# Graph network with slotted neighbours: 36 slots in five PSUM banks, norms computed on ScalarE

## What is computed

```python
def _genconv(h, edge_attr, src, dst, w1, b1, g1, bb1, w2, b2, t):
    msg = jax.nn.relu(h[src] + edge_attr) + EPS_MSG
    m = msg * t
    seg_max = jax.lax.stop_gradient(jax.ops.segment_max(m, dst, num_segments=N))
    ex = jnp.exp(m - seg_max[dst])
    denom = jax.ops.segment_sum(ex, dst, num_segments=N)
    alpha = ex / (denom[dst] + 1e-16)
    agg = jax.ops.segment_sum(msg * alpha, dst, num_segments=N)
    out = h + agg
    z = jax.nn.relu(_layernorm(out @ w1 + b1, g1, bb1))
    return z @ w2 + b2
...
for i in range(1, L):
    z = jax.nn.relu(_layernorm(h, ln_g[i], ln_b[i]))
    h = h + _genconv(z, e, src, dst, ...)
return jax.nn.relu(_layernorm(h, ln_g[0], ln_b[0]))
```

## Time and profile before

| | us |
|---|---|
| median of 3 runs | 6207.28 (6206.5 to 6214.1) |
| the profiled execution | 6218.0 |
| its span, first to last instruction | 6213.7 |
| VectorE busy | 4593.2 (74%) |
| TensorE busy | 4575.7 (74%) |
| GpSimd busy | 4185.6 (67%) |
| ScalarE busy | 2450.6 (39%) |
| mean granted TensorE clock | 0.827 |

### The profile page before, as it was taken

One profiled execution on the slowest core, in us unless ns is written; L12 is line 12 of the kernel. 1 busy time (PEld: TensorE's weight loads), 2 busy tenths in 40 slices (PEclk: granted clock), 3 DMA queues, 4 the chain that ended last, 5 costly groups with the idle time before them and its releaser, 6 DMA issues. The chain is left out here.

```text
span 6213.7 us, 106997 instructions
## 1 busy us (share of the span) xinstructions
PE 4575.7 (74%) x43556; PEld 3238.2 (52%) x43557; DVE 4593.2 (74%) x7210; ACT 2450.6 (39%) x3848; POOL 4185.6 (67%) x3850
## 2 busy tenths in 40 slices
PE   7715888999938777783777877468777756777786
PEld 6715777888825444452445544244544533454443
DVE  9431555444438999994899999489999957888887
ACT  2403566654513444441444443234434423333333
POOL 3054777766547777774777777377777747777775
PEclk8955888666669998896899889789988978898888
DMA  8971777665564555544455555445555534454552
GB/s 344 417 239 66 260 275 282 221 234 221 194 192 167 180 174 185 177 164 118 157 178 183 175 176 177 126 144 179 170 183 177 184 130 136 165 173 165 169 173 88
DMA packets 323285, 1168.13 MB, mean 188 GB/s; under 512 B 142130, under 2 KB 145380, under 8 KB 255444
## 3 DMA queue, kind: packets, MB, share of 16 engines
q1 hardware_dynamic: 172852, 890.91, 38.7%
q0 software_dynamic: 134800, 214.63, 13.7%
q10 hardware_dynamic: 15120, 55.50, 2.2%
HBM read 910.82 MB, written 249.92 MB: 187 GB/s over the span
## 5 line engine op out<-in xcount | busy, mean ns | idle before, releaser
L1258 POOL DMA_INDIRECT gb<-ztab,ovi x2704 | 2945.6, 1089 | 1025.3 <-issue 833.6
L1356 PE MATMUL bank<-ep_mid,keep 128*128 128x512 f32 (+3 forms) x3474 | 1568.1, 610 | 18.8 <-DVE ep_mid L1346 18.8
L1356 PEld LDWEIGHTS bank<-ep_mid,keep 128*128 128x128 f32 x3474 | 699.3, 203 | 853.1 <-issue 820.7
L1309 DVE TENSOR_REDUCE mx<-xb 128x64 f32<-128x2816 f32 (+17 forms) x196 | 1016.7, 5187 | 3.6
L1273 PE MATMUL bank<-zpw,oh_layers 128*128 128x64 bf16 x28812 | 879.7, 194 | 155.9 <-DMA zpw<-ztab 155.9
L1273 PEld LDWEIGHTS bank<-zpw,oh_layers 128*128 128x128 bf16 x28812 | 874.3, 98 | 211.1 <-DMA zpw<-ztab 156.9
L1096 POOL DMA_INDIRECT ecell<-zpw,ptg x588 | 646.8, 1100 | 228.1 <-issue 176.7
L1404 PE MATMUL bank<-keep,na 128*128 128x128 f32 x100 | 47.5, 475 | 952.8 <-DVE na L1401 952.8
L925 PE MATMUL bank<-byk,zpw 88*88 88x102 f32 (+13 forms) x4608 | 665.1, 332 | 53.0 <-DVE zpw L906 49.1
L925 PEld LDWEIGHTS bank<-byk,zpw 88*88 88x88 f32 (+13 forms) x4608 | 654.5, 234 | 62.8 <-DVE zpw L906 54.0
L1319 ACT ACTIVATE cm<-top_x,nt 128x64 f32<-128x64 f32 x196 | 68.2, 348 | 1501.4 <-DVE top_x L1313 1484.9
(11 more groups left out here) (222 smaller groups left out, 5784.6 us busy)
## 6 DMA issues: line engine op xcount, KB each, us to landing
oh_layers<-ohd SPq DMA_DIRECT2D x196, 1568.0 KB, 9.8
ea_in<-in_ea SPq DMA_DIRECT2D x101, 512.0 KB, 8.1
enc<-es_out ACTq DMA_DIRECT2D x101, 512.0 KB
cb<-rowc SPq DMA_DIRECT2D x49, 1024.0 KB
gb<-ztab,ovi POOLq DMA_INDIRECT x2704
...
```

The source lines that it names most:

```text
L1258: at["g"][d] = ga_l[d % 2](GP.indirect_dma_start(gb[d % 2][:, 64 * v:64 * v + 64], None, T["ztab"], bass.IndirectOffsetOnAxis(ap=ovi[:, i: ...
L1309: q = V(VE.tensor_reduce(mx[:, 0:64], x_of(d, 0, S.S[d]).rearrange("p (s f) -> p f s", f=64), AX.X, ALU.max))
L1356: q = PE.matmul(both[d % 2][:, 0:w], ident, rows[:, 128 * (c - a):128 * (c - a) + w], start=(c == 0), stop=(c + 4 >= S.S[d]), skip_group_c ...
```

## The change

Eight source blocks more get a slot of their own (23 singles and 13 pairs: 36 slots, in five groups of 8, 8, 8, 8 and 4) and the overflow shrinks: 628 overflow slots in all instead of 676, and 2392 slots instead of 2244 over the 49 tiles. All tiles have then 41 to 57 slots, tile 1 has 72. The groups use five PSUM banks; for the sums over the slots one bank is left, NA and NB share one, and the maximum `top_x` lies in the eighth. The encodings of the fourth group are added by an identity matmul of TensorE before the one-hot matmuls, and ScalarE copies the finished group into `xb`. The norm's arithmetic after the statistics is moved to ScalarE whole, with a table set that holds both Ln and Exp loaded at the start of a layer, and without gaps; the bias matmuls are issued after the waits for ScalarE. `pick` works in chunks of 6 slots. The diff, cut to its core:

```diff
@@ -50,12 +50,12 @@
 self.NN = 128 * self.ND
 assert self.ND == len(OVER) == len(EDGES) == 2 * self.pairs - 1

-self.singles = 15
+self.singles = 23
 self.groups = [(b, 1) for b in range(self.singles)]
 self.groups += [(b, 2) for b in range(self.singles, self.ND, 2)]
 self.G = len(self.groups)
 self.ones = [sum(n for _, n in self.groups[:s]) for s in range(self.G + 1)]
-assert self.ones[-1] == self.ND and self.G == 32
+assert self.ones[-1] == self.ND and self.G == 36

 self.sorted = [d // 2 if d % 2 else self.ND - 1 - d // 2 for d in range(self.ND)]
 self.place = [self.sorted.index(b) for b in range(self.ND)]
...
@@ -239,26 +240,30 @@
     q = V(VE.bn_aggr(mv[:, s, :], st[:, s, :]))
 yield
 vwait(q)
-root, half, by, shift = (nwf[:, i, :] for i in range(4))
-q = V(VE.tensor_scalar(half, mv[:, :, 1], LN_EPS, -0.5, ALU.add, ALU.mult))
-
+root, half, by, shift, less, fix = (nwf[:, i, :] for i in range(6))
 AE.wait_ge(ve_s, q)
-q = A(AE.activation(by, half, ACT.Ln, scale=-2.0))
+q = A(AE.activation(by, mv[:, :, 1], ACT.Ln, bias=eps[:, 0:1]))
+A(AE.activation(half, mv[:, :, 1], ACT.Identity, bias=eps[:, 1:2], scale=-0.5))
+A(AE.activation(less, mv[:, :, 0], ACT.Identity, scale=-1.0))
 AE.wait_ge(ae_s, q)
 q = A(AE.activation(root, by, ACT.Exp, scale=-0.5))
-for _ in range(3):
-    yield "gap"
-VE.wait_ge(ae_s, q)
+AE.wait_ge(ae_s, q)
 for c in (0, 1):
-    q = V(VE.scalar_tensor_tensor(by[:, c:c + 1], root[:, c:c + 1], half[:, c:c + 1],
-                                  root[:, c:c + 1], ALU.mult, ALU.mult))
-yield
-vwait(q)
-q = V(VE.scalar_tensor_tensor(root, by, 1.5, root, ALU.add, ALU.mult))
-yield
-vwait(q)
-q = V(VE.scalar_tensor_tensor(shift, mv[:, :, 0], -1.0, root, ALU.mult, ALU.mult))
-AE.wait_ge(ve_s, q)
+    q = A(AE.activation(by[:, c:c + 1], root[:, c:c + 1], ACT.Identity,
+                        scale=half[:, c:c + 1]))
+AE.wait_ge(ae_s, q)
+for c in (0, 1):
+    q = A(AE.activation(fix[:, c:c + 1], by[:, c:c + 1], ACT.Identity,
+                        bias=eps[:, 2:3], scale=root[:, c:c + 1]))
+AE.wait_ge(ae_s, q)
+for c in (0, 1):
+    q = A(AE.activation(root[:, c:c + 1], root[:, c:c + 1], ACT.Identity,
+                        scale=fix[:, c:c + 1]))
+AE.wait_ge(ae_s, q)
+for c in (0, 1):
+    q = A(AE.activation(shift[:, c:c + 1], less[:, c:c + 1], ACT.Identity,
+                        scale=root[:, c:c + 1]))
+AE.wait_ge(ae_s, q)
 for s in (0, 1):
     q = A(AE.activation(out[:, s, 0:width], src[:, s, 0:width], ACT.Identity,
                         bias=shift[:, s:s + 1], scale=root[:, s:s + 1]))
...
@@ -1110,8 +1116,8 @@
 vwait(k["ptg"][j])
 if j:
     vwait(k["split", S.put[j - 1]])
-for a in range(0, S.S[d], 20):
-    n = min(20, S.S[d] - a)
+for a in range(0, S.S[d], 6):
+    n = min(6, S.S[d] - a)
     now = hit[:, 0:n * KS].rearrange("p (s k) -> p s k", k=KS)
     if a:
         vwait(q)
...
@@ -1198,17 +1204,19 @@
             landed[2](SP.dma_start(oh[:, 1, :], T["ohd"][1]))]

 def layer(number, tag, args):
-    (oh, z, h, npd, wri, dci, outi, ovi, xb, gb, mx, top_x, cm, ds, nt, zb, zr) = args
+    (oh, z, h, npd, wri, dci, outi, ovi, xb, gb, mx, cm, ds, nt, zb, zr) = args
     final = tag == "last"
     P, V, A = fresh()
+    AE.preload_act_table_set("natural_log_exp_and_others")
     lc = ExitStack()
     with lc:
         n_ep, ep_slots = 3, 24
-        n_gp = 4
+        n_gp = 5
         ep = sb("ep_" + tag, [128, n_ep, ep_slots, 128], FP32, lc)
         xg = zr if final else None
-        gps = bank[0:4]
-        both, NA, NB = bank[4:6], bank[6], bank[7]
+        gps = bank[0:5]
+        both, NA, NB = bank[5], bank[6][:, 0:256], bank[6][:, 256:512]
+        top_x = bank[7][:, 0:128].rearrange("p (a f) -> p a f", a=2)
         pk_l = Landed(pk_s)
         ohl_l = [Landed(s) for s in st_s[2:4]]
         zp_l = Landed(st_s[5])
...
@@ -1217,7 +1225,7 @@
 xg_l = [Landed(s) for s in gq_s[6:8]]
 xl_l = [Landed(s) for s in gq_s[8:10]]

-k = {n: {} for n in ("add", "pass", "over", "topx", "sub", "exp", "mul", "sums",
+k = {n: {} for n in ("add", "lift", "pass", "over", "topx", "sub", "exp", "mul", "sums",
                      "fold", "cm", "node")}
 at = {n: {} for n in ("x", "oh", "g", "xg")}

...
@@ -1264,8 +1272,14 @@
 if j == 0 and d >= 2:
     awaits(PE, at["oh"][d])
 if (d, j) in before_pass:
-    PE.wait_ge(ve_s, before_pass[d, j])
-for s in range(8 * j, min(G, 8 * j + 8)):
+    PE.wait_ge(*before_pass[d, j])
+lo, hi = 8 * j, min(G, 8 * j + 8)
+if j in summed:
+    if d:
+        awaits(PE, at["x"][d])
+    PE.matmul(gps[j % n_gp][:, 0:64 * (hi - lo)], ident, x_of(d, lo, hi),
+              start=True, stop=False, skip_group_check=True)
+for s in range(lo, hi):
     b0, n = S.groups[s]
     for b in range(b0, b0 + n):
         at_oh = 128 * (S.ones[s] + b - b0)
...
@@ -1274,7 +1288,7 @@
                 gps[j % n_gp][:, 64 * (s % 8):64 * (s % 8) + 64],
                 oh[:, d % 2, at_oh:at_oh + 128],
                 zp[:, b, 64 * part:64 * part + 64],
-                start=(b == b0 and part == 0),
+                start=(b == b0 and part == 0 and j not in summed),
                 stop=(b == b0 + n - 1 and part == 2), skip_group_check=True)
 k["pass"][d] = P(q)
 k["pass"][d, j] = k["pass"][d]
...
@@ -1284,15 +1298,21 @@
 def add(d, j):
     if j == 0 and d:
         awaits(VE, at["x"][d])
-    VE.wait_ge(pe_s, k["pass"][d, j])
     lo, hi = 8 * j, min(G, 8 * j + 8)
     x = x_of(d, lo, hi)
+    nxt = (d, j + n_gp) if j + n_gp < JS else (d + 1, j % n_gp)
+    if j in summed:
+        AE.wait_ge(pe_s, k["pass"][d, j])
+        k["lift"][d] = A(AE.copy(x, gps[j % n_gp][:, 0:64 * (hi - lo)]))
+        before_pass[nxt] = ae_s, k["lift"][d]
+        return
+    VE.wait_ge(pe_s, k["pass"][d, j])
     k["add"][d] = V(VE.tensor_tensor(x, gps[j % n_gp][:, 0:64 * (hi - lo)], x,
                                      ALU.add))
-    nxt = (d, j + n_gp) if j + n_gp < JS else (d + 1, j % n_gp)
-    before_pass[nxt] = k["add"][d]
+    before_pass[nxt] = ve_s, k["add"][d]

 JS = -(-G // 8)
+summed = (3,)

 def over(d):
     awaits(VE, at["g"][d])
...
@@ -1304,19 +1324,23 @@
 def most(d):

     vwait(max(k["over"][d], k["add"][d]))
+    VE.wait_ge(ae_s, k["lift"][d])
+    top = mx[:, 64 * (d % 2):64 * (d % 2) + 64]
     if d >= 2:
         VE.wait_ge(ae_s, k["cm"][d - 2])
-    q = V(VE.tensor_reduce(mx[:, 0:64], x_of(d, 0, S.S[d]).rearrange(
+    q = V(VE.tensor_reduce(top, x_of(d, 0, S.S[d]).rearrange(
         "p (s f) -> p f s", f=64), AX.X, ALU.max))
     yield
     vwait(q)
-    q = k["topx"][d] = V(VE.tensor_scalar(top_x[:, d % 2, :], mx[:, 0:64], 0.0,
+    q = k["topx"][d] = V(VE.tensor_scalar(top_x[:, d % 2, :], top, 0.0,
                                           None, ALU.max))
     u, i = S.where[d]
     AE.wait_ge(ve_s, q)
     if u >= 2:
         AE.wait_ge(ve_s, k["node", "den"][u - 2])
-    q = A(AE.activation(cm[:, u % 2, i, :], top_x[:, d % 2, :], ACT.Exp,
+    q = A(AE.activation(cm[:, u % 2, i, :], top, ACT.Relu))
+    AE.wait_ge(ae_s, q)
+    q = A(AE.activation(cm[:, u % 2, i, :], cm[:, u % 2, i, :], ACT.Exp,
                         scale=nt[:, 0:1]))
     AE.wait_ge(ae_s, q)
     k["cm"][d] = A(AE.activation(cm[:, u % 2, i, :], cm[:, u % 2, i, :],
...
@@ -1348,12 +1372,12 @@
     x_of(d, a, b).rearrange("p (s f) -> p s f", f=64), 0.0,
     ep[:, r, 0:b - a, 0:64], ALU.max, ALU.mult))
 PE.wait_ge(ve_s, k["mul"][d, i])
-if i == 0 and d >= 2:
-    PE.wait_ge(ve_s, k["fold"][d - 2])
+if i == 0 and d:
+    PE.wait_ge(ve_s, k["fold"][d - 1])
 rows = ep[:, r, :, :].rearrange("p s f -> p (s f)")
 for c in range(a, b, 4):
     w = 128 * min(4, b - c)
-    q = PE.matmul(both[d % 2][:, 0:w], ident, rows[:, 128 * (c - a):128 * (c - a) + w],
+    q = PE.matmul(both[:, 0:w], ident, rows[:, 128 * (c - a):128 * (c - a) + w],
                   start=(c == 0), stop=(c + 4 >= S.S[d]),
                   skip_group_check=True)
 k["sums"][d, i] = P(q)
...
@@ -1405,9 +1429,9 @@
                    na[:, 0, :, :].rearrange("p s f -> p (s f)"), ident))
 AE.wait_ge(pe_s, q)
 q = A(AE.copy(ot[:, :], NB[:, 0:128]))
-PE.matmul(NA[:, 0:256], ident, b1, start=True, stop=False)
 yield
 PE.wait_ge(ae_s, q)
+PE.matmul(NA[:, 0:256], ident, b1, start=True, stop=False)
 q = P(PE.matmul(NA[:, 0:256], ot[:, :], w1, start=False, stop=True))
 yield "linear1"
 VE.wait_ge(pe_s, q)
...
@@ -1417,13 +1441,13 @@
 PE.wait_ge(ae_s, q)
 for s in (0, 1):
     q = P(PE.transpose(NB[:, 128 * s:128 * s + 128], hb[:, s, :], ident))
-PE.matmul(NA[:, 0:128], ident, b2, start=True, stop=False,
-          skip_group_check=True)
 yield "turned"
 AE.wait_ge(pe_s, q)
 q = A(AE.activation(yt[:, :, :], NB[:, 0:256].rearrange(
     "p (s c) -> p s c", s=2), ACT.Relu, bias=bb1, scale=g1))
 PE.wait_ge(ae_s, q)
+PE.matmul(NA[:, 0:128], ident, b2, start=True, stop=False,
+          skip_group_check=True)
 for s in (0, 1):
     q = P(PE.matmul(NA[:, 64 * s:64 * s + 64], yt[:, s, :], w2,
                     start=False, stop=True, skip_group_check=True))
```

(13 more changed lines are left out.)

5 lines of the change are left out of this document (2 added, 3 removed).

## The result

The changed kernel takes **6418.39 us** (median of 4 runs, 6416.14 to 6420.84), the kernel before 6210.69 beside it: a ratio of 1.0335, 95% interval 1.0317 to 1.0352. It is slower by 208 us (207.7). The forecast was 279 us more, 6486, within a range of 6280 to 6640.

What follows compares the result with a forecast made beforehand. No engine is full; TensorE's and VectorE's chains are equally late in a pair's first part, VectorE alone bounds the second. Three layers +250, last +19, table building +10: +279 on 6207.3, so 6486 us, range 6280 to 6640.

Steps and rivals of the forecast that it cites:

- the first part: Tile pair, from the sum into `na` to the add into `h`: 20.0 us before, +2.4 after, TensorE deciding.
- TensorE's terms: Added to 20.0 us in the pair's first part: bias matmuls 0.5 and 0.4, slots 0.66, identity matmul 0.88; 22.4.
- VectorE's path: VectorE's chain in the pair's first part: work unchanged, a new 1.5 us wait for ScalarE's copy, 21.5 us in all.
- costs taken as nothing: One bank for column sums, maximum in PSUM, and the identity matmul's need of `xb`: nothing put on them.
- The chain on ScalarE: The norm's dependent operations after the aggregate, now all on ScalarE: 3.9 us, range 2.9 to 4.6.
- The wait at the gamma product: Pair's second part: the product stands behind only the first add, so VectorE waits 3.2 us for the norm.
- rival C: Table loads stay because the preloaded set is not honoured: chain 2.6 us longer, pair +7.9, total 6920 us; chance 0.04.
- The second part: Tile pair, from the add into `h` to the next sum into `na`, VectorE alone the path: 20.9 us, +1.2.
- The last layer: Pairs 42.6 us with gather waits, then 43.5 without: +0.9 each over 24, -5.6 and +2.5 at the ends, +19.
- The table building: Stage before the layers, bound by TensorE: larger transposes and copies, more `pick` instructions; +10 us, from 0 to +40.
- A: TensorE's restart after its idle stretch gets cheaper, so VectorE's 21.5 decides: pair +2.7, total 6399 us; chance 0.17.
- B: ScalarE's latencies overlap, chain 1.3 us, VectorE's work decides: pair -1.4, total 6036 us, gain below 2.7; chance 0.08.

Runs made afterwards that it cites:

- a_noid: The changed kernel with the fourth group's encodings added by VectorE again, no identity matmul and no ScalarE copy: 6357.61 us, ratio 1.0240.
- a_banks: The changed kernel with a bank each for NA and NB, `top_x` in SBUF, bias matmuls issued ahead of the waits: 6365.18 us, ratio 1.0235.
- b_psum: b_best with one bank for the sums and the maximum in PSUM, taken by ScalarE with a Relu: 5970.79 us, ratio 0.9603.
- b_best: The kernel before with b_pick6's edits, the table set preloaded and one gap instead of three in the norm: 6092.22 us, ratio 0.9808.
- a_topsb: The changed kernel with the maximum `top_x` back in SBUF, nothing else: 6440.49 us, ratio 1.0372.
- b_tab: The kernel before with the table set preloaded at the start of each layer, nothing else: 6195.35 us, ratio 0.9975.
- b_pick6: The kernel before with `pick` in chunks of 6 slots instead of 20 and the larger share of steps (9, not 4): 6159.46 us, ratio 0.9923.
- b_grid: The kernel before with the 36-slot grid, five banks, one sums bank, all groups added by VectorE, old norm, new `pick`: 6275.31 us, ratio 1.0093.
- a_gap3: The changed kernel with the three gaps put back behind the norm's chain on ScalarE: 6254.92 us, ratio 1.0062.

## Why the prediction was right, and where it was off

**What bounds the kernel.** The two chains of the first part were taken as equally late before the change, and TensorE's as the later one after it. a_noid and a_banks bear the second out: both shortened TensorE's chain, a_noid while giving VectorE more work, the first part shrank by 0.8 and 0.6, and VectorE still waits for TensorE at its end.

**TensorE's terms.** 22.4 was worked out and 22.4 measured for tiles 27 and 28; in the mean it is 22.16, +2.2 instead of +2.4. VectorE's path was to be 21.5; less its wait it was 22.39 - 1.10 = 21.3. The wait before the maximum was put at 1.5 and is 1.36. Of the costs taken as nothing, two don't show: with one bank of sums b_psum has the same first part as b_best (19.97 and 19.96), and a_topsb's pairs are those of the changed kernel (44.2 to 44.4 in the mean over a middle layer, against 44.3). The third does, but not in the pairs that were summed: the identity matmul waited for `xb` in the first two tiles of each layer (67.5 us in eight waits) and nowhere else.

**The chain on ScalarE.** 3.9 was predicted, 3.75 measured. In detail: an operation without a pointer operand took 0.19, with one 0.28 to 0.30, with two 0.38; pairs overlapped by 0.1, and dependent ones followed 0.03 after. The wait at the gamma product was put at 3.2 and is 3.05. The Trainium skill (ScalarE: Activation LUTs, What ACT_TABLE_LOAD costs) gives figures by which I estimated 3.7, and the trace's 3.75 agrees. One reading was wrong: the chain of before, 4.0 us, has one table load in it and not two (the other runs ahead of it in both parts of the pair), as the rows at b_tab show. The forecast didn't use it, but rival C did, which put both loads (2.6 us) on the path.

**The second part.** +1.2 was predicted, +0.96 measured (21.88 against 20.92). Over the second and third layer the 24 pairs grew by 76 us together, 3.2 each and not 3.6, which is 10 less than the 86.4 of the sum. The stretch ahead of the first sum into `na` became 2 us shorter, where the sum had 5.6 for four gathers, and what follows the last one became 1.3 longer, where it had 2.5. So these layers were put 8 us too high. In the first layer the pairs grew by 79.4, but the stretch ahead of them became 11.6 shorter, for a reason that no run shows, and the layer was put 14 too high.

**The last layer.** +19 was predicted, +11.9 measured, for the reason given: its pairs follow their own path now, and only the first gather is waited for (28.5 us). It was mis-sized at both ends: over the 24 pairs the mean was 42.8 before where the sum had 42.6, and 43.4 after where it had 43.5. That is 14 us more in place of 21.6.

**The table building is the term that failed**, in its sign: "+10, from 0 to +40" was -30. The step took TensorE as the bound and VectorE's extra instructions as a price on the side. b_pick6 shows that the shorter chunks with the larger share are a gain of 51. The traces show how TensorE fared, not why: more clock, and VectorE's waits for it (`zpw` on L906) down from 406 to 280 us between 600 and 1720. The cause stays open. The grid then costs part of it. In seven kernels with 36 slots the layers started at 1728.9 to 1760.8 (mean 1743.9), in three with 32 slots and short chunks at 1707.7 to 1721.5 (mean 1713.9): +30. What was on record for the grid here, +5% of transposes and copies, has the right sign. The spread of these starts is 14 us and more for one and the same building, and the latest of them (b_grid and a_gap3 in the first group, b_best in the second) come from profiled executions 18 to 27 us above their medians. So the -30 of the changed kernel's profile is the favourable end; by the means it is -15.

**The rivals.** A (TensorE's restart cheaper) is out: behind the idle 6.82 us the clock is 0.50 again, as in the earlier trace rows:

```profile
3581.00:3583.00 2.00, 1.65 (x4) 1.18 (x5) 2.00 (x2) 0.27 (x1) 1.70 (x2) 0.50 0.20 33
```

B needed a chain under 2.7 us; it is 3.75. C needed table loads in the pairs; there are none, only the one at the start of each layer.

The forecast was 68 us too high: 40 from the building, 31 from the three layers, 7 from the last, 78 in all (77 unrounded). The errors of the five stages all lie on the same side, so none of them hides another, and the two largest terms, the two parts of the pair, came out close. Of the 77, 6 came back because the medians lie further apart than the profiled executions (207.7 against 201.8), and 3 because the median of before is 6210.7 here.

**Taken together.** By the medians, the new `pick` with its share is worth -51, the grid with its five banks +116, and the norms, group four and the shared bank together +143. Within that last sum single edits overlap: taking out group four gains 61, the banks 53, the norm 235, and the gaps alone 163.
